# Maxima by quarters, layout transfers in seven portions, sums behind the rows and narrow value products in a decoder layer with 16 heads of 8

## The reference, cut to what matters

```
x = x + self_attention(layernorm(x))          # 4 batches, 512 rows, 16 heads of 8, rotary
x = x + cross_attention(layernorm(x), ctx)    # ctx: 4 x 32 rows of 64
x = x + ffn(layernorm(x))                     # 6 layers: windowed attention + gated FFN

scores = einsum('bhqd,bhkd->bhqk', q, k) / sqrt(8)
attn = softmax(scores, axis=-1)
out = einsum('bhqk,bhkd->bhqd', attn, v)      # then @ Wo.T

# cross attention, per batch
attn = softmax(einsum('bqhd,bkhd->bhqk', Q, K) * SCALE)
O = einsum('bhqk,bkhd->bqhd', attn, V).reshape(B, xN, 128)   # then @ Wo.T
```

## Time and profile before

| | |
|---|---|
| median of 3 runs | 2017.09 us (2014.5 to 2019.48) |
| the profiled execution | 2019.15 us |
| its span | 2017.3 us |
| self-attention | 0 to 252 us |
| cross attention | 252 to 347 us |
| layers | 347 to 2017 us |
| PE busy | 1912.3 us, 95% |
| DVE, ACT, POOL busy | 80%, 65%, 50% |
| mean granted clock of PE | 0.984 |

### The profile page before, as it was taken

How to read it: one execution, slowest core, us unless ns; L and a number is a source line. 1 busy time by engine, 2 the same in 40 slices (tenths; PEclk the granted TensorE clock), 3 DMA queues, 4 the chain that set the end, 5 groups by cost and what they waited for, 6 DMA issues and landing times.

```text
span 2017.3 us, 46975 instructions
## 1 busy us (share of the span) xinstructions
PE 1912.3 (95%) x19006; PEld 1152.2 (57%) x19006; DVE 1621.9 (80%) x1822; ACT 1304.4 (65%) x1864; POOL 1016.6 (50%) x743
## 2 busy tenths in 40 slices
PE   6799788899999999999999999999999999999987
PEld 3222145566666666666666666666666666666656
DVE  5898256788888888898889888888888898879773
ACT  3398734567666766676667667766776676667754
POOL 6201133665555555555555556555655565556440
PEclk9899999899999999999999999999999999999999
DMA  3340010354433453335443335443445343343431
GB/s 112 68 78 11 13 40 27 88 135 114 106 94 102 126 136 89 98 100 130 123 105 104 102 97 140 110 109 91 114 121 130 93 104 94 103 124 94 110 104 36
DMA packets 106070, 195.55 MB, mean 97 GB/s; under 512 B 14432, under 2 KB 34912, under 8 KB 105600
## 3 DMA queue, kind: packets, MB, share of 16 engines
q1 hardware_dynamic: 105856, 192.55, 37.0%
HBM read 124.49 MB, written 54.79 MB: 89 GB/s over the span
## 4 chain that ended last, share of the span: by engine, by line
PE 69%; DVE 6%; issue 5%; POOL 2%; ACT 1%; POOLq 0%; ACTq 0%; DVEq 0%
PE ps L1518 13%; PE ps L1598 8%; PE ps L1527 8%; PE ps L1587 8%; PE ps L1542 6%; PE ps L1619 6%; PE ps L1564 6%; PE ps L1575 4%; PE ps L1552 4%; PE ps L1631 3%; DVE l_norms L1934 1%; PE ps L1606 1%; DVE l_o_tok L2002 1%; DVE l_mx L1982 1%; DVE l_rot_s L1955 1%
## 5 line engine op out<-in xcount | busy, mean ns | idle before, releaser
L1491 POOL TENSOR_TENSOR l_rot<-l_rot,l_rot_s 128x1024 f32<-128x1024 f32 x192 | 455.6, 2373 | 27.5 <-DVE l_rot_s L1955 27.5
L1480 POOL COPY l_kb<-l_kb 128x512 f32<-128x512 f32 x95 | 61.5, 647 | 641.9 <-ACT l_kb L1773 641.9
L1494 POOL TENSOR_TENSOR l_rot<-l_rot,l_norms 128x1024 f32<-128x1024 f32 x192 | 365.6, 1904 | 15.1
L1747 ACT ACTIVATE l_sq<-ps 128x1024 f32<-128x1024 f32 x192 | 196.2, 1023 | 183.0 <-PE ps L1518 178.6
L1943 DVE TENSOR_TENSOR l_rot<-ps,l_tab_c 128x1024 f32<-128x1024 f32 x192 | 233.7, 1217 | 36.8 <-ACT l_sq L1747 36.8
L1955 DVE TENSOR_TENSOR l_rot_s<-ps,l_tab_s 128x512 f32<-128x512 f32 x384 | 245.6, 681 | 0.0
L1934 DVE TENSOR_REDUCE l_norms<-l_sq 128x16 f32<-128x1024 f32 x192 | 232.2, 1209 | 0.0
L1542 PEld LDWEIGHTS ps<-l_kb,l_qT 128*32 128x32 f32 x6144 | 163.1, 110 | 76.0 <-issue 44.1
L1773 ACT ACTIVATE l_kb<-ps 64x1024 f32<-64x1024 f32 x192 | 195.5, 1018 | 1.7 <-PE ps L1527 0.6
L1542 PE MATMUL ps<-l_kb,l_qT 128*32 128x128 f32 x6144 | 189.0, 275 | 3.8 <-issue 2.9
L1564 PE MATMUL ps<-l_vb,l_pT 128*32 128x128 f32 x6144 | 188.2, 273 | 3.9 <-issue 2.2
(11 more groups left out here) (191 smaller groups left out, 3238.3 us busy)
## 6 DMA issues: line engine op xcount, KB each, us to landing
l_vb<-v_scratch SPq DMA_DIRECT2D x336, 256.0 KB, 4.8
v_scratch<-l_v_tok SPq DMA_DIRECT2D x96, 512.0 KB, 6.0
l_vb<-v_scratch SPq DMA_DIRECT2D x48, 192.0 KB, 3.2
xsT<-xT SPq DMA_DIRECT2D x48, 135.8 KB, 2.5
l_xf<-xT SPq DMA_DIRECT2D x46, 128.0 KB, 2.3
stack<-scratch SPq DMA_DIRECT2D x72, 64.0 KB
l_wqkv_odd<-wqkv SPq DMA_DIRECT2D x9, 512.0 KB, 6.6
scratch<-parts SPq DMA_DIRECT2D x12, 256.0 KB, 5.6
```

What stands on the lines that cost most here:

```text
L1491: nc.gpsimd.tensor_tensor(rot[:, t % 2, n], rot[:, t % 2, n], rot_s[:, n], ALU.add).then_inc(added, 1)
L1494: nc.gpsimd.tensor_tensor(rot[:, t % 2, n], rot[:, t % 2, n], norms[:, t % 2, n, :, None].broadcast_to([P, HEADS, DH]), ALU.mult).then_inc ...
L1747: nc.scalar.activation(sq[:, 1 - r], slot(name, t).rearrange("p n (h d) -> p (n h) d", d=DH), ACT.Square).then_inc(squared, 1)
```

## The change

The maxima are handled by quarters of a batch (PER = 4, HALVES = 16, NM = 16), so AHEAD falls from 48 to 32 products. Each step of the handling (split, turning, copy, store, rows) happens twice as often on half as much. The bulk transfers stand behind the row transfers of a quarter, in seven portions. spread_inverse is cut in two: gather_sums, behind the rows of the quarters 7, 11 and 15, and the rest, behind the rows of the quarters 8 and 12 and at the end. POOL does the last batch's add, rest and low, and the setting of inv to one, behind its first split_max. In the cross attention each group's value product has only its own 32 columns and writes its own 32 partitions.

```diff
-        add(3)
         low(2)
-        rest(3)
-        low(3)
+        def last_parts():
+            add(LAST)
+            rest(LAST)
+            low(LAST)
+        return last_parts
...
-    HALVES = 2 * BATCH
-    NM = TILES * HEADS // 2
+    PER = 4
+    HALVES = PER * BATCH
+    NM = TILES * HEADS // PER
...
-    def spread_inverse(sp, b):
+    def gather_sums(sp, b):
         sp.wait_ge(o_read, GROUPS * (b + 1))
...
+    def spread_inverse(sp, b):
         sp.wait_ge(inv_out, b + 1)
         sp.dma_start(sums_scratch[b], small[:, b, :]).then_inc(inv_in, 16)
...
-        pool.memset(inv[:, :, :], 1.0).then_inc(inv_set, 1)
         for half in range(HALVES):
             split_max(half)
-            if half >= 4 and (half % 2 == 0 or half == HALVES - 1):
-                b = (half + 1) // 2 - 2
+            if half == 0:
+                last_parts()
+                pool.memset(inv[:, :, :], 1.0).then_inc(inv_set, 1)
+            if half > 2 * PER and half % PER == 1 or half == HALVES - 1:
+                b = (half + 2) // PER - 2
                 pool.wait_ge(inv_in, 16 * (9 * b + 9))
...
         for half in range(HALVES):
-            if half == 1:
-                lay_out(sp, 1, 1)
-                lay_out(sp, 1, 2)
-                store(sp, 2)
-            if half == 2:
-                lay_out(sp, 2, 0)
-                lay_out(sp, 2, 1)
-                store(sp, 3)
-            if half == 3:
-                lay_out(sp, 2, 2)
-                lay_out(sp, 3, 0)
-            b, h = divmod(half, 2)
+            b, h = divmod(half, PER)
             sp.wait_ge(m_read, slot_of[half, "turn"] + 1)
             sp.dma_start(max_scratch[half], mrows[:, :]).then_inc(m_stored, 16)
...
+            if half == 0:
+                lay_out(sp, 1, 1)
+                lay_out(sp, 1, 2)
+            if half == 1:
+                store(sp, 2)
+            if half == 2:
+                lay_out(sp, 2, 0)
             if half == 3:
+                lay_out(sp, 2, 1)
+                lay_out(sp, 2, 2)
+            if half == 4:
+                store(sp, 3)
+            if half == 5:
+                lay_out(sp, 3, 0)
+            if half == 6:
                 lay_out(sp, 3, 1)
                 lay_out(sp, 3, 2)
-            if half >= 3 and half % 2:
-                spread_inverse(sp, half // 2 - 1)
+            if half > PER and half % PER == 0:
+                spread_inverse(sp, half // PER - 2)
+            if half > PER and half % PER == PER - 1:
+                gather_sums(sp, half // PER - 1)
+        spread_inverse(sp, BATCH - 2)
...
-                        m = nc.tensor.matmul(ps[:, 7, i * P:(i + 1) * P], vb[:, b, g, :], pT[:, g, i * P:(i + 1) * P],
-                                             start=(g == 0), stop=(g == GROUPS - 1))
+                        own = slice(32 * g, 32 * g + 32)
+                        m = nc.tensor.matmul(ps[own, 7, i * P:(i + 1) * P], vb[:, b, g, own], pT[:, g, i * P:(i + 1) * P],
+                                             start=True, stop=True, skip_group_check=True)
```

More of the change, by code:

```diff
@@ L133, in _ @@
                 def _(pool):
-                    project["gpsimd"](pool)
-                    softmax["gpsimd"](pool)
+                    last_parts = project["gpsimd"](pool)
+                    softmax["gpsimd"](pool, last_parts)
                 @block.tensor
@@ L555, in spread_inverse, with gpsimd @@
                          .broadcast_to([DK, GROUPS, SEQ])).then_inc(inv_in, 16)
-    def gpsimd(pool):
+    def gpsimd(pool, last_parts):
         def split_max(half):
@@ L597, in sync @@
                     r = 64 * parity + MAX_ROW + part
-                    sp.dma_start(stack[r:r + 1, b, 0, 4 * h:4 * h + 4, :].rearrange("o c (i q) -> o (c i) q", q=P),
+                    sp.dma_start(stack[r:r + 1, b, 0, PAIRS // PER * h:PAIRS // PER * (h + 1), :].rearrange("o c (i q) -> o (c i) q", q=P),
                                  max_scratch[half, a:a + NM // 2, :].rearrange("(o n) q -> o n q", o=1))\
                         .then_inc(laid, 16)
-            if half == 3:
+            if half == 0:
[5 more added lines that the diff above has]
+                lay_out(sp, 2, 0)
+            if half == 3:
+                lay_out(sp, 2, 1)
[5 more added lines that the diff above has]
+            if half == 6:
                 lay_out(sp, 3, 1)
                 lay_out(sp, 3, 2)
-            if half >= 3 and half % 2:
-                spread_inverse(sp, half // 2 - 1)
+            if half > PER and half % PER == 0:
[3 more added lines that the diff above has]
+        spread_inverse(sp, BATCH - 2)
     def tensor(pe, last_product, last_products_read):
         def max_scores(half, n):
-            b, c, i, parity = half // 2, 4 * (half % 2) + n // 8, n // 2 % TILES, 1 - n % 2
+            b, c, i, parity = half // PER, PAIRS // PER * (half % PER) + n // 8, n // 2 % TILES, 1 - n % 2
             slot = slot_of[half, n // 2]
@@ L615, in max_scores @@
             if n == 0:
-                pe.wait_ge(*parts_laid[half])
+                pe.wait_ge(*parts_laid[2 * half // PER])
             m = nc.tensor.matmul(ps[:, 2 * (slot % 2) + parity, :], stack[rows(h), b, 0, c, i * P:(i + 1) * P],
@@ L2227 @@
     scratch = nc.dram_tensor("scratch", (BATCH, P, 3, 2, SEQ), BF16, kind="Internal").ap()
-    max_scratch = nc.dram_tensor("max_scratch", (2 * BATCH, P // 2, P), BF16, kind="Internal").ap()
+    max_scratch = nc.dram_tensor("max_scratch", (4 * BATCH, P // 4, P), BF16, kind="Internal").ap()
     sums_scratch = nc.dram_tensor("sums_scratch", (BATCH, P, 4 * GROUPS * SEQ // P), F32, kind="Internal").ap()
```

## The result

The changed kernel takes 2001.26 us (median of four runs, 1996.27 to 2005.08) against 2017.32 us; the ratio is 0.992, 95% interval 0.9893 to 0.9946. That is 16 us, 0.8%, faster where 22 were forecast, and the interval doesn't reach 1, so the gain is clear of the noise. A second set of five runs gave 1999.37 us, ratio 0.9907 (0.9891 to 0.9923).

The account below looks back on a forecast made before the run. The loop of scores, exponentials and values was taken to bound the softmax loop, with stalls from queued transfers. Terms -11.1 - 10.7 + 4.5 + 0.5 - 5.5 = -22.3 us gave 1995 us from 2017.1; range 1985 to 2009.

Parts of the forecast that it names:

- Head: Start of self-attention: the first turning waits only for a quarter's reduction, first score 11.1 us earlier; bounds 9.2 to 13.5.
- Sums behind the rows: Softmax loop: the store of maxima no longer stands behind just-issued broadcasts of the sums; both stalls go, -10.7 us.
- C: Rival: broadcasts or a late inversion keep back the store of quarters 9 and 13, +10.7 us; time 2013; chance 0.07.
- Round trip and slack: The maxima's trip from split through store to rows takes 6.5 us, leaving each quarter 2.7 us of slack.
- B: Rival: rows late in every quarter, PE standing before nearly all; 2035 us at 2 us per quarter; chance 0.06.
- Bulk in seven portions: Maxima's stores queue behind layout portions draining in about 10 us; quarters 4 and 7 late; +4.5 us (0 to +12).
- rival A: Rival: twelve layouts drain in 12 us or more, quarters 3 to 7 all stand; gain 13, time 2004; chance 0.16.
- Eight more turnings: Self-attention: PE turns 16 times instead of 8, +0.5 us; upper bound +5 if DVE's copies come on the path.
- Sums of batch 0 and 1: Self-attention: DVE's inversion comes one quarter later, behind quarter 8's turned maxima; 0 to +2 us, taken as 0.
- End of the stage: End of self-attention: POOL's last product ends 0.2 us before the last output; cost 0, up to +2 us.
- Cross attention: Narrow value products: a tile's eight records take 0.27 us instead of 0.89; -5.5 us, between 0 and -8.
- The layers: Long part the change doesn't touch: starts earlier, takes as long as before; a difference above 2 us would be unforeseen.

Follow-up runs that it names:

- version by halves: Kernel before, maxima still by halves, with the sums gathered and spread behind the rows of halves, and narrow value products: 2000.73 us, ratio 0.9916.
- planned version: Changed kernel with bulk portions of at most ten layouts, nine in succession, and batch 2's sums gathered behind quarter 14 instead of 15: 1989.22 us, then 1992.03 us.

## Why the prediction was right or wrong

- *Head.* Forecast -11.1, measured -11.6 in this pair of profiles. The mechanism is right: the same chain, started by an earlier turning. That the size fits so well is in part luck. In nine profiles of versions with quarters the first score comes at 67.5 to 74.8, on average 72.8, and in four with halves at 79.8 to 83.5, on average 81.9. That is 9.1 us, at the forecast's lower bound. The wait of 2.48 us in front of the turning didn't go either; 1.87 are left. From the first turning to the first score it is 9.8 us here and 10.7 to 10.9 in six of the eight other profiles with quarters, instead of 9.4. No run takes the parts of the head apart.
- *Sums behind the rows.* Forecast -10.7. The two long halves are gone here and in the version by halves, where they alone explain 10.3 us. Right, C falls.
- *Round trip and slack.* Right: without layouts no quarter is late, so B falls. A store of half the size is read back in 1.36 us (164.12 to 165.48), a whole one took 1.73: a little less, far from half. The Trainium skill ("DMA: Bandwidth & Descriptors", section "Anatomy of one DMA — SWDGE (gpsimd) path") has a fixed part of about 2 us that dominates small transfers issued by POOL; the trace agrees that most of the time doesn't go with the bytes, with a lower figure on SP's queue, and with 1.9 us for the stores that POOL issued.
- *Bulk in seven portions.* This is the term that was mis-sized: forecast +4.5, measured +11.0 in the profiled run and +6.3 in the second. The mechanism is as forecast, and the late quarters are 4 and 7 most of all, then 3 and 6. Two sizes were off. First the drain: the DMA share falls to nothing 10.8, 10.1, 11.6 and 11.0 us behind the first issue of the four portions that held a store up, not after "about 10", and the store is read back 1.3 to 1.4 us behind that. PE stands 1.4, 2.5, 0.6 and 3.5 us before the quarters 3, 4, 6 and 7, where my walk had 0.2 us in hand, 2.3 late, 0.4 in hand and 2.1 late: 8.0 us instead of 4.4. Second, I charged a microsecond of standing as one, although show 5.3 lost for 3.5. The two short waits cost what they lasted (1.5 and 0.7 us), but the two long ones 4.3 and 4.6 us, and around the end of the wait at quarter 4 the granted clock is 0.50 (114 to 115 us). Even this isn't a fixed price: in the second profile waits of 2.4 and 2.6 us cost 2.5 and 3.8. The profiled run paid rival A's price; the median, 2001, lies between my 1995 and A's 2004.
- *Eight more turnings.* A quarter takes 9.82 us instead of 9.79: 0.5 us over the loop, as forecast.
- *Sums of batch 0 and 1.* Right, no wait beside the late rows.
- *End of the stage.* Forecast 0 with 0.2 us in hand, measured +0.9 (the gap of 1.1 us instead of 0.3 behind ACT's end). The edge was named, its size missed: the gathered sums were inverted 5.4 us behind the gathering's issue (224.36 to 229.75) instead of 3.8. Why they landed later stays open.
- *Cross attention.* Forecast -5.5, measured -4.0 in traces at equal clock, -2.9 in the profiled run, and -3.9 to -5.9 by medians, so the forecast isn't refuted. A narrow group takes 0.35 us and not 0.27. In a row of passing tiles the period fell only from 2.2 to 2.5 us to 2.15, and where two tiles follow each other later in the stage from 2.19 to 1.85. I had counted more than half of DVE's 5.9 us of waiting as gained, and 2.1 were.
- *The layers.* They begin 12.6 us earlier and end 14.0 earlier; the 1.4 us between are within what the layers differ by from run to run (1665 to 1670 us in the thirteen traces). The prediction's limit of 2 us for this part was too narrow: in the changed kernel's second profile the layers are 4.5 us shorter than in the one before.

In sum -11.6 - 10.7 + 11.0 + 0.5 + 0.9 - 2.9 - 1.4 = -14.2 against the 14.0 by which the spans differ. The changed kernel's second profile comes to its 19.8 us by other sizes of four terms: head -8.3, bulk +6.3, cross attention -3.8, layers -4.5. So the sum closes for each pair of profiles, but single terms of it are good to a few microseconds only, and that the whole came out within 6 us of the forecast owes something to terms that offset each other.

## What to carry to other kernels

When a step is cut in half to start earlier, everything queued between two of its turns has half the time to drain; take the drain rate of what stands in front (here 0.8 to 1.0 us per layout of 64 KB, 10.1 to 11.6 for twelve) and size each portion below one period, counting two portions in succession. A latency-bound transfer goes ahead of bulk in the queue, not behind it and not beside it. Price an engine's relief by the waits of the engine behind it, not by the relieved engine's own time.

## What was not expected of the hardware

The granted clock in the first ten microseconds of the cross attention was 0.66, 0.83 or 1.00 in kernels that do the same there, after an idle time of PE of 1 to 2 us at the stage's start and 1.5 us behind its first products; with rows on POOL's queue, after 7.8 us of idle time, it was 0.55. The eight products behind took 5.3 to 6.2 us instead of 3.7. In the planned version's first profile the clock fell once more inside the stage, to 0.50 some 25 us behind its start, and the stage took 93.8 us instead of some 91. Such differences may be part of the 9 us by which the runs of one kernel differ; no run shows how large a part. The stores of maxima on POOL's queue were read back 1.9 us behind their issue in all quarters shown, 2.4 in the first.
